# Loads of wv and wo that wait for the chunk two before, in a sparse-attention and ternary-FFN layer

## What is computed

```python
q, k, v = heads(x @ wq + bq), heads(x @ wk + bk), heads(x @ wv + bv)
scores = einsum('bhqd,bhkd->bhqk', q, k) / sqrt(128)
probs = softmax(scores * mask)      # mask: i % 10 == 0 and i <= j < i + 10
ctx = einsum('bhqk,bhkd->bhqd', probs, v)
x = layernorm(x + ctx @ wo + bo)
h = square(relu(hbitlinear(x, w_up)))
y = layernorm(x + hbitlinear(h, w_down))
```

## Time and profile before

| what | us |
|---|---|
| median of 2 runs | 7613.28 |
| the two runs | 7603.49 and 7623.06 |
| the profiled execution | 7634.24 |
| its span, slowest core (core 2) | 7632.5 |
| its quickest core | 7599.6 |
| PE, DVE, ACT busy | 2950.5, 2291.6, 599.8 |
| wv and wo loads, from the first chunk of block one to the last of the wo loop | 3366.66 to 4464.43 |

### The profile page before, as it was taken

One profiled execution on the slowest core, in us unless ns is written; L12 is line 12 of the kernel. 1 busy time (PEld: TensorE's weight loads), 2 busy tenths in 40 slices (PEclk: granted clock), 3 DMA queues, 4 the chain that ended last, 5 costly groups with the idle time before them and its releaser, 6 DMA issues.

```text
span 7632.5 us, 43144 instructions; the slowest of 8 cores (7599.6 to 7632.5 us)
## 1 busy us (share of the span) xinstructions
PE 2950.5 (39%) x11509; PEld 1403.0 (18%) x11509; DVE 2291.6 (30%) x2818; ACT 599.8 (8%) x1271; POOL 239.2 (3%) x453
## 2 busy tenths in 40 slices
PE   3546455455500000056555564111332333332582
PEld 1212112112000000023444111000221212121240
DVE  2111111111143333310000013566455545556214
ACT  1000000000000000000000101111111111111000
POOL 1000000000100000000000000000000000000000
PEclk8666666666655555557555665555666667675795
DMA  3222222322323333311112121000212122220322
GB/s 114 77 88 72 88 80 72 97 80 70 106 61 91 91 96 95 95 50 66 66 64 82 56 88 56 22 22 22 68 37 56 39 50 50 50 50 11 90 61 78
DMA packets 484931, 516.91 MB, mean 68 GB/s; under 512 B 381389, under 2 KB 382093, under 8 KB 468127
## 3 DMA queue, kind: packets, MB, share of 16 engines
q1 hardware_dynamic: 443580, 358.05, 16.4%
q0 software_dynamic: 41120, 156.11, 6.6%
HBM read 443.48 MB, written 69.47 MB: 67 GB/s over the span
## 4 chain that ended last, share of the span: by engine, by line
PE 32%; DMA 28%; DVE 27%; issue 8%; ACT 4%; DVEq 1%; SPq 0%; ACTq 0%; POOLq 0%; POOL 0%
DMA arena<-wupT 7%; DMA arena<-wdownT 6%; DVE arena L1284 6%; DMA arenab<-wup_int 4%; PE pb L961 4%; PE pb L1660 3%; DMA arena<-wv 3%; DVE arena L1281 3%; PE pb L1467 2%; DVE arenab L447 2%; DVE arena L442 2%; DMA arena<-x_full 2%; DVE arena L1527 2%; PE pb L515 2%; PE pb L927 2%
## 5 line engine op out<-in xcount | busy, mean ns | idle before, releaser
L515 PE MATMUL pb<-arena 128*1 128x512 f32 x512 | 433.0, 970 | 333.0 <-DMA arena<-x_full 284.4
L1600 PE MATMUL pb<-arena 128*128 128x128 f32 x288 | 83.7, 400 | 902.5 <-DVE arena L1290 897.0
L1284 DVE TENSOR_TENSOR arena<-arena 128x2048 f32<-128x2048 f32 (+3 forms) x126 | 423.1, 3358 | 22.5 <-DVE arena L1281 22.5
L847 PE MATMUL pb<-arena 11*128 11x11 f32 x128 | 27.8, 247 | 956.0 <-DVE arena L856 952.9
L1467 PE MATMUL pb<-arenab 128*128 128x256 bf16 (+1 forms) x2048 | 294.9, 308 | 242.4 <-DMA arenab<-wup_int 210.5
L442 DVE TENSOR_TENSOR arena<-arena 128x1024 f32<-128x1024 f32 x128 | 156.9, 1226 | 670.2 <-DMA arena<-wupT 345.5
L961 PE MATMUL pb<-arena 128*128 128x44 f32 (+1 forms) x1536 | 284.6, 364 | 158.1 <-DMA arena<-wv 158.1
L413 DVE TENSOR_REDUCE arena<-arena 128x1 f32<-128x1024 f32 x128 | 156.2, 1220 | 542.3 <-DMA arena<-wupT 283.9
L961 PEld LDWEIGHTS pb<-arena 128*128 128x128 f32 x1536 | 279.2, 285 | 176.2 <-issue 176.2
L557 PE MATMUL pb<-arenab 128*128 128x104 bf16 x256 | 93.7, 366 | 536.9 <-DVE arenab L542 536.9
L1467 PEld LDWEIGHTS pb<-arenab 128*128 128x128 bf16 x2048 | 216.8, 109 | 320.2 <-issue 270.8
(11 more groups left out here) (191 smaller groups left out, 4023.7 us busy)
## 6 DMA issues: line engine op xcount, KB each, us to landing
arena<-x_full POOLq DMA_DIRECT2D x256, 256.0 KB, 3.0
arenab<-wup_int SPq DMA_DIRECT2D x128, 512.0 KB, 4.9
arena<-wupT SPq DMA_DIRECT2D x96, 512.0 KB, 4.0
arena<-wdownT SPq DMA_DIRECT2D x96, 512.0 KB, 3.8
arena<-wv SPq DMA_DIRECT2D x48, 1024.0 KB, 4.7
arena<-xtm POOLq DMA_DIRECT2D x17, 1024.0 KB, 5.2
wup_int<-arenab SPq DMA_DIRECT2D x64, 256.0 KB, 3.1
arena<-wupT POOLq DMA_DIRECT2D x32, 512.0 KB, 4.5
```

Source lines behind the costliest of these rows:

```text
L515: te.matmul(pb[qb][0:1, 0:512], onesc[:, 0:1], cx[par][:, 0:512], start=(tt < 4), stop=(tt >= 252)),
L1284: E("vector", lambda ve: ve.tensor_tensor(w_ap, w_ap, t_ap, AX.add), wait=[(c_ve, None)], inc=[c_ve])
```

## The change

The wait of each wv load is no longer the tensor counter's value of now, but its value at the end of the chunk that used the same buffer last. `wvte` keeps that value for each of the two buffers: it is set after the 16 matmuls of a chunk and carries over from block to block. The wo loop takes it over as `wote` (it has the same two buffers) and sets it after the last L1051 of a chunk. The first two wv loads have the value 0, which is no wait; the barrier ahead of the stage still holds the first of them, and by SP's order also the second.

```diff
--- before.py
+++ after.py
@@ -914,6 +914,7 @@
         ctxz_ve = c_ve.val
         ctx_bank = {2: (c_ve, 0), 3: (c_ve, 0)}
         sv_ve = 0
+        wvte = {0: 0, 1: 0}
         for bi, (w0, nwn) in enumerate(((0, 4), (4, 4), (8, 2))):
             for wi in range(nwn):
                 wdx = w0 + wi
@@ -944,7 +945,7 @@
                 par = cc % 2
                 vc, vv = ld(wvb[par][:, :],
                             wv_d[cc * 128:(cc + 1) * 128, :],
-                            wait=[(c_te, None)], stream=f"wv{par}")
+                            wait=[(c_te, wvte[par])], stream=f"wv{par}")
                 if bi == 0:
                     for ns in range(4):
                         E("tensor", lambda te, cc=cc, ns=ns, par=par:
@@ -968,6 +969,7 @@
                             if (cc == 0 and h == 0) else
                             ([(vc, vv)] if h == 0 else ())),
                       inc=([c_te] if h == NH - 1 else []))
+                wvte[par] = c_te.val
             cmm = c_te.val
             if bi == 0:
                 for ns in range(4):
@@ -1033,10 +1035,11 @@
 
         E("vector", lambda ve: ve.memset(uprime[:, :], 0.0), inc=[c_ve])
         upz = c_ve.val
+        wote = dict(wvte)
         for cc in range(NCH):
             par = cc % 2
             vc, vv = ld(wob[par][:, :], wo_d[cc * 128:(cc + 1) * 128, :],
-                        wait=[(c_te, None)],
+                        wait=[(c_te, wote[par])],
                         stream=f"wo{par}")
             for ns in range(4):
                 E("tensor", lambda te, cc=cc, ns=ns, par=par: te.matmul(
@@ -1070,6 +1073,7 @@
                     out=uprime[tgt:tgt + 1, :], in_=ustg[ui:ui + 1, :]),
                   wait=[(c_se, usev), (c_ve, upz)],
                   inc=[stream_ctr("upr")], incn=16)
+            wote[par] = c_te.val
         bmm = c_te.val
         for ns in range(4):
             E("vector", lambda ve, ns=ns: ve.tensor_copy(
```

## The result

The changed kernel took 7287.17 us (median of 9 runs, 7264.02 to 7305.91) against 7624.58 us for the kernel before (median of 8): the ratio is 0.9557, with a 95% interval of 0.9538 to 0.9577. That is 337.4 us less. The prediction had 335.8 us less. Its 7277.5 us over the 7613.28 us it was made against is a ratio of 0.9559. The profiled execution took 7301.44 us with a span of 7299.8 us, on core 1. The profile of before was of core 2; core 2 of the new profile has nearly the stage of core 1 (V loop 536.5 against 535.4 us, wo loop 195.0 against 195.2). Where a length of the V loop is given, it runs from the first start of L952 to the last of L962; that of the wo loop from the first start of L1054 to the last (L951, L961 and L1051 before).

A forecast was written before the change was run, and what follows sets the result against it. PE stood idle 324.4 us for 64 unhidden 1 MB loads. The terms, 158.2 + 79.2 + 8 + 87.0 − 2.6 + 17 − 6 − 5, sum to 335.8 us less than 7613.28: 7277.5 us, range 7210 to 7350.

The forecast's parts named there:

- (a): Blocks two and three: 32 waits for wv loads go, −158.2 us, with the clock staying at 0.50.
- (b): Block one: 16 waits for wv loads go, −79.2 us, and the swinging clock gives −8 us more.
- the −28 that were its end: Block one, favourable end: L951 runs wholly at clock 1.00, 28 us less.
- some cold ends of L961: Block one: L961 partly falls to clock 0.50, against fewer cold starts of L951; all at 0.50, 53 us more.
- (c): Wo loop: 16 waits go, −87.0 us; corrections +2.6 for a memset, −17 for L1042's clock, +6 for a new wait.
- the new wait: Wo loop: ACT's first copy of a chunk waits for the previous chunk's small transfers from ustg, +6 us, ends 0 and +24.
- (d): Loads now meeting others: +2.5 us each for an xtm load and the small transfer before L1008, +5 us.
- R1: Clock rises everywhere, also in blocks two and three, and the load becomes the bound: about 7168 us, chance 0.07.
- R2: Clock falls and stays down in block one, so nothing is won there: 7364 us, chance 0.09.
- R4: The earlier issue is still not early, as where SP waits on something else: 7613 us, chance 0.03.
- R3: Wv and wo loads on all eight cores slow each other; kernel over 2% slower, chance 0.01.
- a sign of being wrong: Listed beforehand as showing the prediction wrong: landings of wv loads beyond 7 us.

## Why the prediction was right

By its own steps:

- **(a) Blocks two and three, −158.2 us.** Measured: the 32 waits are gone. The two stretches of before were 191.16 and 192.50 us; L962's busy time of the two blocks is now 110.5 (169.9 less block one's 16 x 3.71) and 109.4 us, and there is 0.7 us of idle ahead of each, so about −162. The 4 us more are in the bursts: 7.02 us each when they stood alone, 6.8 to 6.9 now that one follows the other. The clock stayed at 0.50 as the step said. That this comes of the short matmuls and not of something else was only argued there; the kernel with four dense matmuls a chunk shows it.
- **(b) Block one, −87.2 us.** Measured: 221.02 − 122.96 = −98.1. The waits went and L952 fell from 82.7 to 64.9 us, −17.8 of the −28 that were its end, while L962 kept its 3.71 us in all 16 chunks. The step that was mis-sized is "some cold ends of L961": there were none. The mechanism behind it was real, for the clock did fall in unbroken work: within 3423 to 3424 us, at the seam between L962 and L952, with PE busy the whole microsecond. What was wrong is where it falls: at the seam, so that L952 pays and not L962.

```profile
3422.00:3423.00 1.00, 1.00 (x12) 1.00 (x10) 0.00 (x0) 0.00 (x0) 0.00 (x0) 1.00 0.00 0
3423.00:3424.00 1.00, 1.00 (x8) 0.64 (x7) 0.00 (x0) 0.00 (x0) 0.00 (x0) 0.80 0.00 0
3424.00:3425.00 1.00, 1.00 (x2) 0.13 (x1) 0.00 (x0) 0.00 (x0) 0.00 (x0) 0.50 0.50 66
```

- It fell at the start of three chunks after the first, and there the dense L952 paid for it (5.28 instead of 3.59 us) and brought it back before L962 began. The end of 28 us stands on 3.44 us for L951 at 1.00; it measured 3.59.
- **(c) The wo loop, −95.4 us** (87.0 − 2.6 + 17 − 6). Measured from the end of the transpose before the loop to the last L1051: 298.0 us before, 204.2 us now (3922.87 to 4127.05), −93.8. By terms: L1042's idle 87.0 to 2.8 us, −84.2 as foreseen; L1042 itself 91.7 to 70.7, −21 where I had −17; the new wait +7.6 (PE's idle for ACT 43.5 to 51.1), near the 6 I had. The 36.7 us of ACT's idle are not this term, for ACT also stands about 4 us a chunk for PE where no transfer is late. One term was missing: L1051, which I left as it was, went from 77.0 to 81.8, +4.8, for the clock falls behind each new wait. It hid the 4 us that L1042 won beyond my −17, and that is luck. The luck is larger than it looks, because L1051 stood already at 77.0 only on core 2 (75.6 on core 3). On the other six cores of before it took 65.2 us, and now takes 78.9 to 81.8 there. Core 2, then core 0, of before:

```profile
L1051 PE MATMUL pb<-arena 128*2 128x512 f32 x128 | 77.0, 688 | 43.5 <-ACT arena L1059 43.5
```

```profile
L1051 PE MATMUL pb<-arena 128*2 128x512 f32 x128 | 65.2, 590 | 43.5 <-ACT arena L1059 43.5
```

- **(d) Meetings of loads, +5 us.** The xtm load after block two held PE 7.74 us instead of 5.95, the small transfer before L1010 5.42 instead of 2.52: +4.7 for these two. Over all ten xtm waits it is 59.1 to 62.4 us, so +6.2 with the small transfer.

Added up, the stage is about 349 us shorter on the profiled cores, 13 more than the 335.8 of the sum. The spans of these two executions differ by only 332.7 us, because the stage begins 11.3 us later (3366.66 to 3377.95) and the rest of the kernel is some 5 us longer; both vary as much from core to core. So the terms were off by up to 11 us, and that the medians differ by just 337.4 us is in part chance.

R1, the clock that rises everywhere, did not come in the changed kernel, but with dense matmuls spread in the stream core 0 showed its course for block two: the clock at 1.00, and the load as the bound, with 118 instructions in 15 us, which at 40 a chunk is 5.1 us a chunk (I had worked out 4.3). R2 and R4 fell with the first stretch. R3 fell too: 144 GB/s a core moved with a landing of 4.9 us. The longest landing of a wv load was 8.7 us, beyond the 7 us that I had named as a sign of being wrong (6.9 to 8.7 on the eight cores, 5.6 at most before). It cost next to nothing, for PE waited for wv 1.3 us in all at most (core 6) and not at all on the profiled core.

The Trainium skill's rule that a stream without gaps keeps the high clock ("TensorE: Matmul & The Clock Gate", section "Why this matters for your kernels") does not hold here: block three was busy 109.39 of 109.90 us at 0.50, and in block one the clock fell three times with PE busy throughout.

## What to carry to other kernels

Two buffers overlap nothing as long as the load waits for the engine's newest work. Look for a load issued just after the last matmul of the chunk that used the other buffer; the idle time in front of the chunks is then nearly the whole gain, and can be read from the groups. When such a wait goes, look at what shares its moment: a load that now starts together with a small transfer someone waits for should be issued behind it, or the small transfer's source doubled. When you price a new wait, take the idle of the engine that sets the pace and not that of the engine that waits (7.6 and not 36.7 us here), and add what the clock may lose behind it. And a granted clock of 0.50 in a busy stream may be the stream's own doing.

## What had not been expected

- A transfer of 8 KB took 1.6 us when issued ahead of the load and up to 5.2 us beside a load of 1 MB issued about 1.3 us before it; ordering the two was worth 30 us over 15 chunks.
- Seven waits that held PE up by 7.7 us in sum cost 30 us on the path; the other 22.5 were matmuls at the lower clock after them.
- A granted clock can be kept or lost for a whole block by nearly the same stream: with the spread bf16 matmuls core 0 stayed at 1.00 through block two, while core 6 fell behind a wait of 1.35 us for wv and stayed at 0.50 (8.1 instructions a microsecond before the fall, 4.5 after it).
